# Attention: transposed probabilities written back into the scores' own places, a ninth place, and value products taken two pairs at a time, ahead of transposes and scores

## The reference, cut to what matters

```python
q = _split_heads(query_antecedent @ Wq, h) * d_head ** (-0.5)
k = _split_heads(memory_antecedent @ Wk, h)
v = _split_heads(memory_antecedent @ Wv, h)
logits = jnp.einsum('bhqd,bhkd->bhqk', q, k) + bias
weights = jax.nn.softmax(logits, axis=-1)
x = jnp.einsum('bhqk,bhkd->bhqd', weights, v)
```

## Time and profile before

| | us |
|---|---|
| median of 3 runs | 1052.1 |
| lowest and highest run | 1049.76, 1055.27 |
| the profiled execution, its own time | 1050.43 |
| its span in the trace | 1048.7 |
| TensorE busy over the span | 985.9 (94%) |
| VectorE busy | 611.1 (58%) |
| ScalarE busy | 484.5 (46%) |
| granted TensorE clock, mean | 0.978 |

### The profile page before, as it was taken

One profiled execution on the slowest core, in us unless ns is written; L12 is line 12 of the kernel. 1 busy time (PEld: TensorE's weight loads), 2 busy tenths in 40 slices (PEclk: granted clock), 3 DMA queues, 4 the chain that ended last, 5 costly groups with the idle time before them and its releaser, 6 DMA issues.

```text
span 1048.7 us, 17978 instructions
## 1 busy us (share of the span) xinstructions
PE 985.9 (94%) x7218; PEld 798.9 (76%) x7218; DVE 611.1 (58%) x1209; ACT 484.5 (46%) x625; POOL 261.3 (25%) x223
## 2 busy tenths in 40 slices
PE   7899999999999999999999999768869999999995
PEld 6588777888777888777887777343459999989884
DVE  4335986465986466986454984588961112455551
ACT  3111786062786155786151786368711102455551
POOL 0401840001840001840001830588310101111100
PEclk9999999999999999999999999898959999999998
DMA  8182871522871614871421853700059949699930
GB/s 281 40 156 76 191 185 47 203 81 75 192 180 47 264 40 151 191 175 50 150 106 37 195 124 122 283 1 2 23 189 389 377 164 342 206 381 334 329 91 13
DMA packets 76923, 169.91 MB, mean 162 GB/s; under 512 B 6440, under 2 KB 16808, under 8 KB 71968
## 3 DMA queue, kind: packets, MB, share of 16 engines
q1 hardware_dynamic: 74720, 163.87, 51.0%
q0 software_dynamic: 2112, 4.80, 2.0%
HBM read 119.01 MB, written 16.10 MB: 129 GB/s over the span
## 4 chain that ended last, share of the span: by engine, by line
PE 78%; DMA 6%; DVE 6%; POOL 4%; issue 3%; ACT 2%; SPq 1%; POOLq 0%; DVEq 0%; ACTq 0%
PE psum L461 11%; PE psum L2117 9%; PE psum L441 7%; PE psum L476 7%; PE psum L2132 6%; PE psum L380 5%; PE psum L397 5%; PE psum L398 5%; PE psum L399 5%; PE psum L381 5%; PE psum L382 5%; DMA xg<-xm_rows,row_id 3%; PE psum L2149 2%; PE psum L2151 2%; PE psum L2150 2%
## 5 line engine op out<-in xcount | busy, mean ns | idle before, releaser
L883 POOL CAST stack<-kT 128x2048 fp32r<-128x2048 f32 x32 | 64.0, 2006 | 405.3 <-DVE keys_lo L592 393.6
L628 DVE CUSTOM_DVE_ANT_0 prob<-psum,biasmap,top 128x512 f32<-128x512 f32 x192 | 144.2, 751 | 21.4 <-PE psum L441 12.0
L796 ACT ACTIVATE prob<-prob,top 128x2048 f32<-128x2048 f32 x64 | 128.5, 2008 | 27.0 <-DVE top L628 26.6
L461 PE MATMUL psum<-ident,prob 128*128 128x128 f32 x1024 | 134.9, 275 | 1.2 <-issue 0.8
L2117 PE MATMUL psum<-xT,wring 128*128 128x128 f32 (+3 forms) x1024 | 135.1, 293 | 0.6 <-ACT xT L2430 0.6
L2117 PEld LDWEIGHTS psum<-xT,wring 128*128 128x128 f32 x1024 | 132.7, 193 | 1.5 <-ACT xT L2430 0.8
L461 PEld LDWEIGHTS psum<-ident,prob 128*128 128x128 f32 x1024 | 116.3, 141 | 22.1 <-issue 7.5
L758 ACT COPY kT<-psum 128x512 f32<-128x512 f32 x64 | 37.5, 586 | 198.7 <-PE psum L382 191.7
L804 ACT COPY probT<-psum 128x1024 f32<-128x1024 f32 x96 | 96.5, 1010 | 45.6 <-PE psum L476 44.0
L397 PE MATMUL psum<-wv_hi,ctx_part 128*128 128x512 f32 x256 | 100.1, 391 | 0.0
L398 PE MATMUL psum<-wv_lo,ctx_part 128*128 128x512 f32 x256 | 99.8, 390 | 0.0
(11 more groups left out here) (256 smaller groups left out, 1721.1 us busy)
## 6 DMA issues: line engine op xcount, KB each, us to landing
wring<-in_w SPq DMA_DIRECT2D x64, 1024.0 KB, 7.8
ctx_raw<-in_ctx_t SPq DMA_DIRECT2D x15, 1024.0 KB, 6.0
stack<-stack SPq DMA_DIRECT2D x32, 256.0 KB, 4.7
early_stack<-early_stack SPq DMA_DIRECT2D x28, 256.0 KB, 5.2
ternary<-ternary_weights SPq DMA_DIRECT2D x1, 6272.0 KB, 24.7
prob<-in_w_gate_t SPq DMA_DIRECT2D x1, 5632.0 KB, 17.4
stack<-key_stack SPq DMA_DIRECT2D x20, 256.0 KB, 3.9
query_stacks<-prob SPq DMA_DIRECT2D x16, 256.0 KB, 5.4
```

What stands on the lines that cost most here:

```text
L461: mm = pe.transpose(psum[:, w + i, j * P:(j + 1) * P], prob[:, prob_slot(n, j), kt * P:(kt + 1) * P], ident[:, :])
L628: dve.tensor_tensor_reduce(prob[:, slot, keys], psum[:, scores.of[n, j, c], :], biasmap[:, keys], 1.0, top[:, h, (c + 1) % 2:(c + 1) % 2 + ...
L796: act.activation(prob[:, slot, :], prob[:, slot, :], ACT.Exp, bias=top[:, h, 1:2], scale=-1.0, accum_out=top[:, h, 2:3]).then_inc(*raised. ...
```

## The change

Four things are changed together.

1. `probT` is gone. A move writes the transposed pair back over the 1024 numbers of `prob` from which it was made, and W reads it there. A move waits for its T alone, no longer for a W.
2. `prob` has nine places. Quads 0 to 3 of a batch start at places 1, 5, 0 and 4 (`SCORES_AT`), so the third and fourth quad's first head has a place that nobody reads. Their second head waits for `multiplied` of the quad before the last, where before the first head waited for `turned`.
3. In a slot the order on TensorE was S, T, W. It is now W, T, S, where W comes in even steps only, two pairs at once (`weighed_with`): before T(t) stand W(t-4) and W(t-3). `WEIGH_LATER` is 4.
4. `finish` and `spread_sums` move from slot 3 to slot 4 (`FINISH_AT`), the sums from slot 5 to slot 6. SyncE's two loads that waited for `turned` of a last pair wait for `multiplied` of it.

```diff
-WEIGH_LATER = 2
+WEIGH_LATER = 4
-SUMS_AT = 5
+FINISH_AT = 4
+SUMS_AT = 6
...
-        PS = 2 * QUAD
+        PS = 2 * QUAD + 1
-        probT = sb("probT", [P, 2, 2 * QUAD * P], F32, region_r)
...
+        SCORES_AT = (1, 5, 0, 4)
...
+        def weighed_with(t):
+
+            return () if t is None or t % 2 or t < WEIGH_LATER else (t - WEIGH_LATER, t - WEIGH_LATER + 1)
...
         def prob_slot(n, j):
-            return (QUAD * n + j) % PS
+            return SCORES_AT[n % DT] + j
+
+        def pair_place(n, p):
+
+            first = SCORES_AT[n % DT]
+            return prob[:, first:first + QUAD, 2 * p * P:(2 * p + 2) * P].rearrange("p j (i q) -> p i j q", i=2)
...
-            def turn_and_weigh(b, turned_step, weighed_step):
-                if turned_step is not None:
-                    turn_pair(*pair_of_step(b, turned_step))
-                if weighed_step is not None:
-                    multiply_pair(*pair_of_step(b, weighed_step))
+            def weigh_and_turn(b, t):
+                for m in weighed_with(t):
+                    multiply_pair(*pair_of_step(b, m))
+                if t is not None:
+                    turn_pair(*pair_of_step(b, t))
...
                     for i in range(SLOTS_OF_QUAD):
+                        if n > DT * b:
+                            weigh_and_turn(b, step_of_slot(n, i))
                         score_slot(n, i)
...
-                        if n > DT * b:
-                            turn_and_weigh(b, *steps_of_slot(n, i))
...
-                multiply_pair(*pair_of_step(b, STEPS - 2))
+                for m in (STEPS - 4, STEPS - 3):
+                    multiply_pair(*pair_of_step(b, m))
                 if b + 1 < B:
                     project_key_tile(b + 1, 0, 0)
...
-                multiply_pair(*pair_of_step(b, STEPS - 1))
+                for m in (STEPS - 2, STEPS - 1):
+                    multiply_pair(*pair_of_step(b, m))
...
-                elif g >= 2 and j == 0:
-                    dve.wait_ge(*turned.at(n - 2, 2 * c + 1))
+                elif g >= 2 and j == 1:
+                    dve.wait_ge(*multiplied.at(n - 2, 2 * c + 1))
...
-                dve.wait_ge(*multiplied.at(*before))
-                dve.tensor_copy(probT[:, p % 2, :], psum[:, w:w + 2, :].rearrange("p a n -> p (a n)")).then_inc(
-                    *moved_v.made(n, p))
+                dve.tensor_copy(pair_place(n, p), pair_banks(p)).then_inc(*moved_v.made(n, p))
...
-                        if i == 3 and n > DT * b + 1:
+                        if i == FINISH_AT and n > DT * b + 1:
                             finish(n - 2)
...
-                sp.wait_ge(*turned.at(DT * b - 1, LAST))
+                sp.wait_ge(*multiplied.at(DT * b - 1, LAST))
...
-            sp.wait_ge(*turned.at(QUADS - 2, LAST))
+            sp.wait_ge(*multiplied.at(QUADS - 2, LAST))
```

More of the change, by code:

```diff
@@ L197, in perceiver_block @@
         region_r.close()
-        view = lambda slot: prob[:, slot, :].rearrange("p (k n) -> p k n", k=DT)
+        view = lambda slot: prob[:, slot + 1, :].rearrange("p (k n) -> p k n", k=DT)
         wq_sb, wk_sb, wv_sb, xhT, x_in, q_all, q_hi, q_lo = (view(s) for s in range(8))
-        wo_sb, x_again, attended_sb = view(0), view(1), view(2)
+        wo_sb, x_again, attended_sb = view(-1), view(0), view(1)
         prob_flat = prob[:, :, :].rearrange("p s n -> p (s n)")
@@ L337, in stack_place, with pair_banks @@
                 return RING_PLACES[ring_turn(n, j) % len(RING_PLACES)]
-            return early_stack[:, (QUAD * (n - n % DT + 1) + EARLY_AT[n % DT][j]) % PS, :]
+            return early_stack[:, SCORES_AT[1] + EARLY_AT[n % DT][j], :]
         def prob_slot(n, j):
-            return (QUAD * n + j) % PS
+            return SCORES_AT[n % DT] + j
+        def pair_place(n, p):
+            first = SCORES_AT[n % DT]
+            return prob[:, first:first + QUAD, 2 * p * P:(2 * p + 2) * P].rearrange("p j (i q) -> p i j q", i=2)
+        def pair_banks(p):
+            w = pair_bank(p)
+            return psum[:, w:w + 2, :].rearrange("p i (j q) -> p i j q", j=QUAD)
         def raw_piece(b, p):
@@ L474, in multiply_pair @@
                         columns = slice((QUAD * g + j) * DH, (QUAD * g + j + 1) * DH)
-                        at = (kt % 2 * QUAD + j) * P
                         mm = pe.matmul(quad_out[j * DH:(j + 1) * DH, :], v[:, kt, columns],
-                                       probT[:, p % 2, at:at + P], start=(kt == 0), stop=(kt == KTILES - 1),
+                                       prob[:, prob_slot(n, j), kt * P:(kt + 1) * P], start=(kt == 0), stop=(kt == KTILES - 1),
                                        tile_position=(0, j * DH))
@@ L729, in vector_attention @@
                             add_bias(n, j, c)
-                        step = steps_of_slot(n, i)[0] if n > DT * b else None
+                        step = step_of_slot(n, i) if n > DT * b else None
                         if step is not None and by_vector(*pair_of_step(b, step)):
                             move_pair(*pair_of_step(b, step))
-                        if i == 3 and n > DT * b + 1:
+                        if i == FINISH_AT and n > DT * b + 1:
                             finish(n - 2)
-                        if i == 3 and n > DT * b:
+                        if i == FINISH_AT and n > DT * b:
                             spread_sums(n - 1)
@@ L799, in move_pair @@
             def move_pair(n, p):
-                w = pair_bank(p)
                 act.wait_ge(*turned.at(n, p))
[L802 to L805, removed]
+                act.copy(pair_place(n, p), pair_banks(p)).then_inc(*moved_a.made(n, p))
             for k in range(DT):
@@ L894, in gpsimd_attention @@
             pool.wait_ge(*slice_low.at(DT - 1, "wk"))
-            pool.memset(prob[:, 1, :], 0.0).then_inc(*constants.made("zeros"))
+            pool.memset(prob[:, 2, :], 0.0).then_inc(*constants.made("zeros"))
             for n in quads:
@@ L917, in store_queries @@
                 sp.wait_ge(*constants.at("zeros"))
-                zeros = prob[:, 1, :].rearrange("p (k n) -> p k n", k=DT)
+                zeros = prob[:, 2, :].rearrange("p (k n) -> p k n", k=DT)
                 for j in range(QUAD):
```

10 lines of the change are left out of this document (3 added, 7 removed).

## The result

| | before | after |
|---|---|---|
| median of 4 runs, us | 1052.57 | 1064.32 |
| lowest and highest, us | 1049.76, 1055.27 | 1063.72, 1066.15 |
| the profiled execution, own time and span, us | 1050.43, 1048.7 | 1064.82, 1063.0 |
| third quad of the last batch, us | 16.92 | 18.59 |

The ratio is 1.0115, with a 95% interval of 1.0085 to 1.0145: the change makes the kernel 1.1% slower. The forecast was 1055.0, with a range to 1063: right in its sign, short by 9 us in size, and the result lies outside the range. Part of the 9 is the base: the forecast stands on a median of 1052.1, and the 73 later runs of the kernel before, in three series, have one of 1054.3.

The account below looks back on a forecast made before the run. TensorE, busy 94% of the span, was taken to set the pace. A batch gains 5.1 us and loses 5.6; three times 0.5 plus 1.4 for the last batch makes +2.9 on 1052.1, so 1055.0 us, range 1041 to 1063.

Parts of the forecast that it names:

- TensorE's part: TensorE's instruction prices alone: two slots take 3.85 us against 4.21, a gain of 5.1 us a batch with the tail.
- the walk: Step-by-step timing of the third quad: waits of 0.48, 0.51, 0.44 and 0.30 us, quad 17.35 instead of 16.92.
- S to c0: Time from a slot's start of S to VectorE's first bias unit, taken as 0.64 us throughout.
- T(4): Transpose in a batch's second quad, forecast to wait 0.93 us for ScalarE's move 2.
- the second head's new wait: Third and fourth quads: the second head's wait for multiplied of W(6,7), ending at 7.39 us, was forecast free.
- The step that failed: VectorE's finish with spread_sums, now in slot 4, was priced at 0.55 us to the next unit.
- The last batch's chain: From W(23) through stored output and reload to the next stage's finish, 22.2 us later: moves with W(23) alone, batch +1.4 us.
- The tail's gain: Two tail steps take 2.90 us instead of 3.20, a gain of 0.30; mostly hidden in the last batch.
- TensorE's pace: Rival: fewer changeovers pay in full and the forecast waits don't come; 19.5 us faster, 1033 us, chance 0.12.
- ScalarE's loop: Rival: ScalarE's exponential and moves become the bound once c3 or a handoff is over 0.24 us late; 1063 us, chance 0.22.

Follow-up runs that it names:

- e3: The changed kernel with the old order S, T, W, one W a slot, and finish and sums in their old slots: 1052.79 us, ratio 0.999.
- e9: The changed kernel with each GpSimd cast of 2048 numbers a partition cut into four of 512: 1053.79 us, ratio 1.0.
- e10: The changed kernel with FINISH_AT put back from 4 to 3, the sums staying in slot 6: 1052.44 us, ratio 0.9995.
- e5: The changed kernel with the copy of spread_sums made by ScalarE, one slot later, in place of VectorE: 1051.14 us, ratio 0.9962.
- e8: The changed kernel with ScalarE making the spread_sums copy and all moves within slots, order W, S, T, and sums in slot 7: 1037.32 us, ratio 0.9834.
- e6: The changed kernel with ScalarE making every move within slots, VectorE keeping three moves of the tail: 1052.08 us, ratio 0.997.
- e11: The kernel before with ScalarE making the spread_sums copy and all moves within slots, and sums in slot 7: 1054.01 us, ratio 0.9998.
- e12: e8 with the order W, T, S in a slot in place of W, S, T: 1044.85 us, ratio 0.9912.

## Why the prediction was right and wrong

**TensorE's part was right.** 3.85 us for two slots is the sum of the rows: joined W 1.01 (1.01), T behind W 0.85 (0.86), S 0.55, T 0.79, S ahead of W 0.64 (0.64, which no row of before had shown). T followed by S pays nothing extra, 0.79 and 0.55. The Trainium skill's rule against which the rows were weighed (TensorE: Matmul & The Clock Gate, section "The mechanism"), taken by itself, doesn't hold here; the same section also lets a load go ahead when it targets the background weight buffer, and the measured prices agree with that.

**The waits of the walk came, where nothing held VectorE.** TensorE's timeline in the fourth quad, where there are no casts:

```profile
639.23 0.71 PE L453 MATMUL psum<-stack,qstack 128*128 128x512 f32 x2
640.18 1.09 PE L473 MATMUL psum<-ident,prob 128*128 128x128 f32 x8 [0.24 <-DVE prob L648]
...
644.88 0.71 PE L453 MATMUL psum<-stack,qstack 128*128 128x512 f32 x2
645.90 1.08 PE L487 MATMUL psum<-prob,v 128*32 128x128 f32 x32 [0.31 <-DVE oT L671]
...
648.31 0.27 PE L496 MATMUL psum<-ident,inverse 128*128 128x128 f32 x1
648.75 1.09 PE L473 MATMUL psum<-ident,prob 128*128 128x128 f32 x8 [0.17 <-DVE prob L648]
649.60 1.06 PE L453 MATMUL psum<-stack,qstack 128*128 128x512 f32 x2
650.59 1.08 PE L487 MATMUL psum<-prob,v 128*32 128x128 f32 x32
```

By the same prices as above these are waits of 0.40, 0.38, 0.36 and 0.35 for T(17), W(16), T(21) and slot 7's bank, forecast 0.48, 0.51, 0.44 and 0.30. That the first three are some 0.1 shorter has its reason in the number of which the prediction was least sure: S to c0, 0.64 before, is 0.52 where S follows T (624.95 to 625.47). The quad takes 17.07 (651.60, the start of T(22), and 0.86, less 635.39), forecast 17.35. In the second quad T(4) waits 0.81 for ScalarE's move, forecast 0.93. That in-place moves are free, and the second head's new wait too, is e3's result.

**The step that failed** is the price of `spread_sums` in slot 4: "finish with spread_sums 0.55 to the next unit", taken from the earlier trace rows where the copy stood in slot 3. The term was carried to its new place unchanged; there it measured 2.08 (626.88 to 628.96) in every third quad, while in the fourth, without a cast, it is 0.54 (645.47 to 646.01), as forecast. In second quads the copy took 1.1 to 1.3. The walk asked of VectorE's instructions only what they wait for and what stands behind them on VectorE, and never what GpSimd does at that moment. The cast can't be seen in any wait of VectorE: it makes its instruction longer, and the engine isn't idle. In the third quad the waits come to 3.03 us where the walk has 1.73. In the second T(5) waits 0.81 for a move behind the held copy, of which the walk has nothing.

**By size.** The starts of batches in the two traces differ by 1.9, 2.7 and 2.1 us a batch, and the last batch up to the output projection by 2.9; forecast 0.5 and 1.4. So attention lost 9.5 us where 2.9 was forecast, in the mean 1.65 more a batch. The last batch's quads account for it: the third is 1.24 over the walk (18.59 against 17.35), T(5)'s wait 0.81, the fourth 0.28 under it, and T(4)'s wait 0.12 under, 1.65 together. With the hold shortened or taken away in three ways, e9, e10 and e5, the kernel stands at ratios of 1.0, 0.9995 and 0.9962; 2.9 us would be 1.0028. e9, which leaves VectorE as it is, is the cleanest, and lies a little below the forecast, as the shorter waits would have it.

**The last batch's chain was right.** W(23)'s place ends 13.87 us later than before (657.42 against 643.55), and the finish that opens the next stage 13.78 later (679.55 against 665.77 in the earlier trace rows). The tail's gain behind W(23) is hidden.

**The rivals.** TensorE's pace, 19.5 us of gain, is what e8 comes near (17.5) once VectorE and the order are out of the way, and not what the change did. ScalarE's loop (1063) names nearly the measured time, by luck. Its condition, c3 over 0.24 us late, was met in slot 5 of the third quads, but by the hold, and the cause isn't ScalarE's. Two rows of the table of waits (us in total, times, longest), transposes' weight loads in the changed kernel:

```profile
PEld psum L473 <- DVE prob L648: 14.9, 20, 0.9
...
PEld psum L473 <- ACT prob L810: 8.2, 20, 1.3
```

They wait more for VectorE's moves than for ScalarE's, of which there are more, and e6, which loads ScalarE further, is 12 us faster.

**What stays open.** Of the 11.75 us between the medians, attention accounts for 9.5. The profiled executions differ by 14.4, of which 4.3 arise ahead of attention's first score. Busy time by window from 20 to 60 us, after:

```profile
20.00:60.00 40.00, 35.40 (x117) 22.20 (x116) 15.14 (x21) 5.36 (x10) 10.51 (x10) 0.87 0.15 51
```

The granted clock is 0.87 there, and was 1.00 before. e11, in the old order, has 0.87 too and starts attention at 110.38 us (after 110.22, before 105.89), and e9, e10 and e12, with joined W, have no such delay (106.2 to 106.7); the others lie between. So it varies from run to run, and isn't the change. The mean clock of whole runs says how much it may bear on the medians: the four runs of the changed kernel have 0.970 to 0.976, and 56 runs of the kernel before in that range, in the three series, took 1051.7 to 1057.6, 1054.5 in the mean. That is 10.1 below the changed kernel's mean of 1064.6, near attention's 9.5. What sets the clock in that stretch stays open.

## What to carry to other kernels

An instruction's price belongs to the place where it was measured. When one is moved, look at what each other engine does at the new place, those without a semaphore between them too: here a long GpSimd operation on SBUF made a small VectorE copy there as long as what was left of it, and a product of two SBUF operands too. The sign in a profile is one line with two durations (0.23 and 1.76 us here), and an engine that is busier in one of two equal stretches. And where an order on the busiest engine gives a gain that doesn't show, ask which queue stands behind its handoffs: here the joined products were worth 17.5 us, but only once VectorE had no moves in the slots, the copy was on ScalarE, and scores went ahead of transposes (9 without the last).

## What the runs showed of the hardware

- VectorE's copy (128x4 spread to 128x128, within SBUF) ended 0.07 to 0.09 us after the end of the GpSimd instruction that ran as it began: 1.76 us with 1.68 of a cast left, 0.48 with 0.40 left, 0.23 with none. GpSimd's subtraction did the same: 0.755 us with 0.67 of it left, in the kernel before. `tensor_tensor` with both inputs in SBUF was held alike (1.82 against 0.29, ending 0.14 behind the cast).
- Not held by the same casts: VectorE's reciprocal of 128x4 within SBUF (0.17 us, begun 0.01 into a cast, and 0.17 well inside one, at 609.06), `finish`, with one input in PSUM (0.29, at 611.92 in a cast of 610.38 to 612.28, before), moves from PSUM (1.22, begun at 611.83 in a cast of 610.30 to 612.22), and ScalarE's copy within SBUF (0.30).
- A cast of 2048 numbers a partition took 1.90 us, four of 512 took 2.29 together. Shorter instructions cost GpSimd 0.4 us and saved VectorE 1.28.
